# Identity multiplies in TensorE's idle stretches of a sort

## Time and profile before

| | |
|---|---|
| median of 3 runs | 3935.76 us (3934.3 to 3937.07) |
| profiled execution, its own time | 3940.46 us |
| its span, first to last instruction | 3938.5 us |
| mean granted TensorE clock | 0.762 of full speed |
| busy: TensorE, VectorE, ScalarE, GpSimd | 50%, 57%, 30%, 63% of the span |

### The profile page before, as it was taken

How to read it: one execution, slowest core, us unless ns; L and a number is a source line. 1 busy time by engine, 2 the same in 40 slices (tenths; PEclk the granted TensorE clock), 3 DMA queues, 4 the chain that set the end, 5 groups by cost and what they waited for, 6 DMA issues and landing times. The chain is left out here.

```text
span 3938.5 us, 28658 instructions
## 1 busy us (share of the span) xinstructions
PE 1959.2 (50%) x7633; PEld 850.9 (22%) x7633; DVE 2236.6 (57%) x3952; ACT 1172.2 (30%) x1736; POOL 2467.8 (63%) x2477
## 2 busy tenths in 40 slices
PE   0441119998876868686865036785863300000034
PEld 0111113333222323232322012332321100000023
DVE  8889987887567666767677555544322020210355
ACT  0120005554543434343433024553553300000000
POOL 1000007776777777777777777777777777777573
PEclk9975558998987989897977568997987755555567
DMA  4110004543443434444431433232332310111133
GB/s 110 26 26 0 0 11 76 100 77 69 76 70 77 78 73 75 83 71 77 81 60 27 78 51 78 67 86 69 86 112 52 111 28 10 28 10 27 39 116 127
DMA packets 651925, 247.81 MB, mean 63 GB/s; under 512 B 552260, under 2 KB 632564, under 8 KB 649332
## 3 DMA queue, kind: packets, MB, share of 16 engines
q1 hardware_dynamic: 573844, 216.69, 23.4%
q0 software_dynamic: 77920, 29.29, 7.2%
HBM read 152.62 MB, written 91.71 MB: 62 GB/s over the span
## 5 line engine op out<-in xcount | busy, mean ns | idle before, releaser
L796 POOL DMA_INDIRECT ring<-table,src_i x2048 | 2023.7, 988 | 661.2 <-issue 546.9
L766 POOL DMA_INDIRECT ring<-keys_d,place x128 | 147.7, 1154 | 627.6 <-DVEq L1269 587.5
L1625 DVE TENSOR_TENSOR_SCAN ad<-ns,cad,raw 128x128 f32<-128x128 f32 (+2 forms) x68 | 26.5, 451 | 745.6 <-DMA ring<-table,src_i 745.5
L1003 PE MATMUL ps<-arena 64*128 64x512 f32 x800 | 219.2, 670 | 396.8 <-DMA arena<-xnT 259.7
L898 PE MATMUL ps<-arena,w 64*128 64x448 f32 x896 | 255.4, 650 | 185.8 <-DVE arena L1668 114.6
L1050 PE MATMUL ps<-ident,ends 128*20 128x128 f32 x6 | 1.5, 414 | 596.3 <-DVEq L1865 596.3
L1123 ACT ACTIVATE ex<-ex 128x1024 f32<-128x1024 f32 (+2 forms) x17 | 17.1, 1006 | 831.0 <-DVE ex L1640 831.0
L1200 ACT ACTIVATE arena<-ps,arena 128x1024 f32<-128x1024 f32 x200 | 213.0, 1115 | 116.9 <-PE ps L1003 116.8
L1668 DVE TENSOR_TENSOR arena<-arena,ps 128x448 f32<-128x448 f32 x297 | 172.1, 616 | 115.5 <-ACT ps L1117 115.3
L911 PE MATMUL ps<-arena,w 128*64 128x448 f32 x896 | 216.5, 606 | 39.3 <-issue 39.3
L1117 ACT ACTIVATE ps<-ps,tb 128x448 f32<-128x448 f32 x297 | 169.6, 605 | 210.1 <-PE ps L898 190.2
(11 more groups left out here) (346 smaller groups left out, 3952.1 us busy)
## 6 DMA issues: line engine op xcount, KB each, us to landing
arena<-in_x SPq DMA_DIRECT2D x304, 110.0 KB
ring<-table,src_i POOLq DMA_INDIRECT x2048
partial<-res SPq DMA_DIRECT2D x15, 1536.0 KB, 6.1
arena<-in_x SPq DMA_DIRECT2D x160, 140.0 KB
outputs_d<-arena SPq DMA_DIRECT2D x32, 512.0 KB, 2.8
arena<-outputs_d SPq DMA_DIRECT2D x32, 512.0 KB, 4.9
arena<-xnT SPq DMA_DIRECT2D x100, 128.0 KB, 3.1
arena<-h_tok SPq DMA_DIRECT2D x50, 256.0 KB
```

The lines of the kernel that those rows point to most:

```text
L766: g.indirect_dma_start(out=blocks[:, k, :], out_offset=None, in_=keys_d[:, :], in_offset=off(ap=place[:, k:k + 1], axis=0)).then_inc(done, 16)
L796: g.indirect_dma_start(out=ring[k % 2][:, j - FROM[k], :], out_offset=None, in_=table[0:GRAPH_NODES, :], in_offset=off(ap=src_i[:, j:j + 1 ...
L1003: m = mm(hid[ee % 2][:, z * NT:(z + 1) * NT], fw1[lower_upper(z), ee, :], xf[q][lower_upper(z), :], start=True, stop=True)
```

## The change

TensorE gets a function `busy(b, n)` that multiplies the 128x128 identity by the 128x512 weight tile `w2`, n times, into PSUM bank b. Nothing reads the results and no semaphore is raised by them. It is called in three places. In `sort_turns`, ahead of the wait of each burst: 0 times before forward half 1, 13 times before forward half 0, and 3p times before each back half of phase p (91 and 126 calls over the seven phases). Behind the sort, after a wait for the new semaphore `nearly_sorted`, 26 times before the product of samples; VectorE raises it with a no-op when four stages of the last seven are left. And 6 times between the row-base product and the product for the previous row. In all 249 calls.

```diff
 SORT_AT = 4
 SEARCH_AT = 12
+BUSY_FROM = 4
+BUSY = 26
+BUSY_ROWS = 6
+BETWEEN = [lambda p: 0, lambda p: 13, lambda p: 3 * p, lambda p: 3 * p]
...
+            def busy(b, n):
+
+                for i in range(n):
+                    mm(bank(b), ident[:, :], w2[:, :], start=True, stop=True)
+
             def sort_turns():
...
                 for n in range(28):
                     phase, back, half = n // 4, n // 2 % 2, 1 - n % 2
+                    busy(4 * back, BETWEEN[n % 4](phase))
                     pe.wait_ge(S["half_turned"] if back else S["sorted_part"], n // 4 * 2 + n % 2 + 1)
...
+                pe.wait_ge(S["nearly_sorted"], 1)
+                busy(4, BUSY)
                 for b in range(4):
                     pe.wait_ge(S["samples_ready"], b + 1)
...
                 mm(bank(2)[:, 0:1], above, incl[:, P - 1:P], start=True, stop=True).then_inc(S["rowbase_done"], 1)
+                busy(4, BUSY_ROWS)
                 pe.wait_ge(S["prev_ready"], 1)
...
                         for b in range(7, 0, -1):
+                            if b == BUSY_FROM:
+                                v.nop().then_inc(S["nearly_sorted"], 1)
                             stage_all(2 ** b)
```

More of the change, by code:

```diff
@@ L339, in build @@
         names = """consts pads_zero edges_in weights_in cls_ps cls_sb cls_in cls_st par_act par_dve wp1
-            turned sorted_part half_turned upper_copied prev_ready prev_done prev_read keys_st samples_ready samples_read hist_done
+            turned nearly_sorted sorted_part half_turned upper_copied prev_ready prev_done prev_read keys_st samples_ready samples_read hist_done
             rowbase_in rowbase_done wide_ready search_ready search0 search1 starts_found shifted starts_ready starts_st ends_in place_f_ready
```

## The result

The kernel with the change takes 4021.54 us (median of 5 runs, 4013.97 to 4022.36) against 3937.07 us for the kernel before on the same chip: a ratio of 1.021, with a 95% interval of 1.0196 to 1.0224. By the ratio it is 83 us slower (the two medians are 84.5 us apart): clearly slower, with an interval that lies on both sides of 2%. 4012 us was forecast.

A forecast was written before the change was run, and what follows sets the result against it. GpSimd's nearly fixed gather stream, started by `search_ready`, was taken to bound the kernel. Phases 68 + 3.5 and samples 5.1 us gave 76.6 us on the median of 3935.76: 4012 us, range 3999 to 4040.

The forecast's parts named there:

- What bounds the kernel: GpSimd's gathers start at `search_ready`, behind sort and samples, then run a nearly fixed stream; any delay there moves the end equally.
- The rival of a delay that is not carried: Something unshifted holds GpSimd's stream behind the sort, so the time stays within 8 us, about 3936 us; 3 in 100.
- The price of one filler: One `busy` call over 512 columns takes 0.86 us at the high clock level and about 1.75 us at the low one.
- The rival of cheap fillers: A filler costs 0.43 us, all fit their waits; bursts gain 5.5 us and samples 6 us, 3924 us; 10 in 100.
- The turning point: At about 0.55 us a filler, growth of the 6p fillers between the bursts eats up the gain from cheap fillers.
- When the clock rises: TensorE's clock rises 4.7 us after a restart from idle (ends 3.35 and 7.9), losing 2.35 us; transposes count towards it.
- The rival of a clock that never rises: A filler takes 1.75 us, the seven stretches 431 us against 163, samples start 33 us late: about 4236 us; 3 in 100.
- The phases: In the sort, TensorE's queue ends last from phase 1 on: six phases 68 us later, phase 0 3.5 us later.
- The formula 17.8 + 5.16p: Stretch in us from first burst to VectorE's restart in sort phase p: 23.0 in phase 1, 48.8 in phase 6.
- Behind the fourth-last stage: The 26 fillers start the product of samples 11.7 us late; faster batches make its end 5.1 us late, upper end 11.7.
- Behind the row-base product: Six fillers, 5.2 us, delay the front, which runs up to 4.0 us faster: zero taken, between -4 and +5.
- The sum: 68 + 3.5 + 5.1 = 76.6 us later at `search_ready`, carried one for one to the end: 4012 us, 1.9% slower.

The follow-up runs named there:

- e2: The change with only the fillers between the bursts, none behind the sort: 4001.94 us, ratio 1.0159 to the kernel before.
- e7: The change with only the 3p fillers ahead of each back burst: ratio 1.0125 to the kernel before.
- e10: The change with only the fillers between the bursts, each over 384 columns instead of 512: ratio 1.0044 to the kernel before.
- e12: The change with only the 26 fillers behind the fourth-last stage: 3948.9 us, ratio 1.0032 to the kernel before.
- e1: The change with all 249 fillers, each over 256 columns instead of 512: 3934.37 us, ratio 0.9987 to the kernel before.
- e9: The change with only the fillers between the bursts, each over 256 columns instead of 512: 3928.85 us, ratio 0.9985 to the kernel before.
- e4: e1 with the one-hot tiles laid out so that each multiply of the product of samples reads neighbouring elements: ratio 0.9994 to the kernel before.
- e11: The change with only the six fillers behind the row-base product: ratio 1.0013 to the kernel before.
- e3: The change with only the 26 and the six fillers behind the sort, none between the bursts: 3961.15 us, ratio 1.0053.

## Why the prediction was right, and where it was not

**What bounds the kernel.** Right. What `search_ready` lost the end lost: 78.2 us at the first gather, 83 (77 to 88) in time for the change, and the same in e2, e7, e10 and e12 within their intervals. The rival of a delay that is not carried is out. The distance from the first search gather to the end is not as fixed as the prediction has it: 3337.1 us before and 3344.2 in the change, and 3332.0 to 3353.9 over the profiled executions.

**The price of one filler.** Right: 0.858 us measured, 0.86 from the rows of another line with half the columns. The rival of cheap fillers is settled by e1 and e9: at 0.43 us the counts of the diff do fit, and the gain is 6 us in the phases; the 6 us that the rival had in the samples do not come. The diff's counts suit that price; at 0.86 us they are twice too many. The turning point that the prediction put near 0.55 us lies between 0.43 (-6) and 0.64 us (+20).

**When the clock rises.** The slow start was put at 2.35 us lost. From the first burst to the second, against 12.15 us if all were fast (1.0 + 13 x 0.858), the seven phases took 13.4 to 15.0 us: 1.3 to 2.9 us lost, 2.0 on average. The rival of a clock that never rises is out. That transposes count towards the rise is seen again in phase 0 of e7, which has no fillers: sixteen transposes took 3.61 us there, and the next eight 1.10 us.

```profile
273.74 3.61 PE L863 MATMUL ps<-ident,res 128*128 128x128 f32 x16 [8.20 <-DVE res L1348]
277.78 1.10 PE L863 MATMUL ps<-ident,res 128*128 128x128 f32 x8 [0.43 <-DVEq L1327]
```

The Trainium skill ("TensorE: Matmul & The Clock Gate", Part 4: PE-mode transpose) says that the full rate does not engage for transposes; this trace and that of before show that it does.

**The phases.** 68 + 3.5 were forecast, 66.3 measured. The formula 17.8 + 5.16p gave 23.0 and 48.8 us for phases 1 and 6; measured were 21.5 and 48.8. The shorter slow starts are about half of the difference (14.0 us lost in the seven phases, not 16.5). Most of the rest is the burst: a fast one takes 0.87 us from start to start (315.40 to 316.27), where the formula has 1.0.

**Behind the fourth-last stage.** This step failed. The fillers took 24.9 us as forecast (24.75), but "at the high level each of its four batches takes half of 3.88 us" was wrong: a multiply took 0.24 us at either clock, the product 15.46 us, and nothing was made up. 11.9 us were lost from the last restart to the first gather, not 5.1. The upper end that the prediction kept, 11.7 us, had the right size for a wrong reason: the clock did fall, but what held the product up was operands read at a stride (e4). The row of before showed the product busy at 0.50, and I took its time for the clock's without a row at the other level.

**Behind the row-base product.** Zero was taken, with -4 to +5 as bounds; e11 measured 5 us (2 to 9), of which 2.6 show in GpSimd's wait. The prediction looked at `search_ready` alone; VectorE, which gives `place_ready` later, does stand behind the six.

**The sum.** 76.6 forecast, 78.2 at the first gather. Phases 5 us too high and samples 7 us too low nearly cancel, so the sum is better than its terms, and that is luck. In time it was 83 us; the excess over the first gather is about what e11 shows for the six.

## What to carry to other kernels

A filler that keeps TensorE's clock up stands in the same queue as the work it is meant to serve, so it is free only as long as the group of fillers, at the price of a row of the same type and with the slow start, is shorter than the wait it stands in. Price it from records per call and start-to-start distances, and ask of each stretch that is to profit whether its time halved in any row at the higher clock; the product that reads its operands at a stride did not. Here 256 columns instead of 512 turned 2.1% slower into 0.13% faster (e1), and 0.15% without the calls behind the sort (e9).

## What was not expected of the hardware

- A bf16 multiply of 128 x 128 by 128 columns that reads both operands 32 bytes apart takes 0.24 us whether the granted clock is 1.00 or 0.50; with neighbouring elements about 0.06 and 0.11 us. The Trainium skill ("SBUF — State Buffer", Door 1: The DMA port swizzle) says that an access which goes to a new 16-byte line each time, 8 bf16 elements, pays a penalty; e4 agrees in kind, and puts a factor of 4 on it at the high clock and 2 at the low one.
- During that product the granted clock fell from 1.00 to 0.50 between 3.3 and 4.0 us after its start, with TensorE shown as busy all that time (in the change, in e1, in e3 and in e12). The moments are worked out from the mean granted clock of short stretches; why it fell is not shown. The Trainium skill ("TensorE: Matmul & The Clock Gate", Why this matters for your kernels) names idle gaps as what drops the clock; here it dropped without one that the profile shows.
- VectorE writes a 128 x 2048 bf16 tile in 1.22 us to neighbours and in 9.2 us when the elements lie 256 bytes apart.
- The gather stream scatters: from its first to its last gather it took 2690.6 us (e10) to 2710.5 us (e3) in the profiled executions, and the first burst of the sort began between 263.5 and 269.0 us, in step with no edit. Effects of a few us are therefore read at marks inside the trace.
